# The first half step of a two-level matrix kernel by eight plain block products instead of seven, and where two token sums are made

## The reference, cut to what matters

```python
# x: (2, 2048, 512) fp32; wi[e], swi[k]: 512 x 2048; wo[e], swo[k]: 2048 x 512
s0 = relu(x @ swi[0]) @ swo[0]
s1 = relu(x @ swi[1]) @ swo[1]
eo = relu(x @ wi[type_label]) @ wo[type_label]      # one expert for each batch entry
w  = softmax(relu(concat(eo[:, 0], s0[:, 0], s1[:, 0]) @ g1) @ g2)
x  = x + eo * w0 + s0 * w1 + s1 * w2
x  = x + (x @ W[cat_ids] + b[cat_ids])
```

## Time and profile before

| | |
|---|---|
| median of three runs | 1970.01 us |
| profiled execution, device time | 1970.03 us |
| its span, first to last instruction | 1968.2 us |
| mean granted clock of TensorE | 0.994 of full |
| PE busy | 1938.7 us (99%) |
| DVE busy | 1338.0 us (68%) |
| ACT busy | 982.4 us (50%) |
| POOL busy | 525.2 us (27%) |

### The profile page before, as it was taken

The page is one execution under the profiler, slowest core; times in us unless marked ns, Lnnn a source line. Parts: engine busy times, 40 slices in busy tenths (PEclk is TensorE's granted clock), DMA queues, the critical chain, the costliest instruction groups (busy, mean ns, idle before and its releaser), DMA issues.

```text
span 1968.2 us, 25213 instructions
## 1 busy us (share of the span) xinstructions
PE 1938.7 (99%) x8504; PEld 1598.9 (81%) x8504; DVE 1338.0 (68%) x1391; ACT 982.4 (50%) x1438; POOL 525.2 (27%) x399
## 2 busy tenths in 40 slices
PE   6999999998999999999999999999999999999999
PEld 5888888887888888888888888888878888888887
DVE  7888788899566565555755554579985665565556
ACT  6666766665453433344554444456655533344342
POOL 5546545553121111111211111254531111111120
PEclk8999999999999999999999999999999999999999
DMA  6776667766876666666776676678767776656652
GB/s 219 257 260 263 257 256 288 278 240 253 286 243 215 215 212 212 189 196 194 247 257 206 193 227 199 202 258 297 268 232 264 247 235 205 216 182 211 230 160 96
DMA packets 187026, 450.99 MB, mean 229 GB/s; under 512 B 16916, under 2 KB 57876, under 8 KB 180500
## 3 DMA queue, kind: packets, MB, share of 16 engines
q1 hardware_dynamic: 186900, 449.39, 67.5%
HBM read 308.81 MB, written 140.51 MB: 228 GB/s over the span
## 4 chain that ended last, share of the span: by engine, by line
PE 95%; DVE 3%; DMA 1%; issue 1%; ACT 1%; POOL 0%; SPq 0%; DVEq 0%; ACTq 0%; POOLq 0%
PE ups L1351 46%; PE rps L1351 45%; PE aps L1351 3%; DMA XT<-in_x_dram 1%; DVE XT L604 0%; DVE XL L996 0%; DMA XS<-in_x_dram 0%; DVE WU L1005 0%; DVE HT L623 0%; DVE HL L1025 0%; DVE ACC L1044 0%; ACT HH L814 0%; DVE WD L1012 0%; DVE XT L1308 0%; ACT WD L752 0%
## 5 line engine op out<-in xcount | busy, mean ns | idle before, releaser
L1351 PE MATMUL ups<-XH,WU 128*128 128x512 f32 x2688 | 891.3, 392 | 24.6 <-DVE WU L1005 9.0
L1351 PE MATMUL rps<-HH,WD 128*128 128x512 f32 x2672 | 877.5, 389 | 0.6 <-ACT rps L829 0.6
L1351 PEld LDWEIGHTS ups<-XH,WU 128*128 128x128 f32 x2688 | 508.0, 189 | 137.4 <-ACT u L774 9.5
L1351 PEld LDWEIGHTS rps<-HH,WD 128*128 128x128 f32 x2672 | 502.4, 188 | 106.1 <-DVE HL L1025 1.3
L1351 PE MATMUL ups<-XL,WU 128*128 128x512 f32 x1344 | 526.1, 391 | 0.0
L1351 PE MATMUL rps<-HL,WD 128*128 128x512 f32 x1336 | 520.3, 389 | 0.0
L623 POOL TENSOR_TENSOR HT<-hid 128x512 f32<-128x512 f32 x96 | 135.1, 1408 | 998.8 <-PE rps L1351 998.8
L1025 DVE TENSOR_TENSOR HL<-HT,HH 128x1024 fp32r<-128x1024 f32 x240 | 306.2, 1286 | 9.2 <-ACT HH L814 5.1
L1351 PEld LDWEIGHTS ups<-XL,WU 128*128 128x128 f32 x1344 | 254.1, 189 | 52.2
L1351 PEld LDWEIGHTS rps<-HL,WD 128*128 128x128 f32 x1336 | 251.3, 188 | 52.2
L1047 DVE SCALAR_TENSOR_TENSOR ACC<-rps,gw,ACC 128x1024 f32<-128x1024 f32 x126 | 161.6, 1282 | 191.7 <-PE rps L1351 191.5
(11 more groups left out here) (113 smaller groups left out, 1574.3 us busy)
## 6 DMA issues: line engine op xcount, KB each, us to landing
WU<-wu_kept SPq DMA_DIRECT2D x448, 256.0 KB, 3.3
WD<-wd_kept SPq DMA_DIRECT2D x224, 512.0 KB, 3.3
wd_kept<-WD SPq DMA_DIRECT2D x112, 512.0 KB, 3.1
wu_kept<-WU SPq DMA_DIRECT2D x32, 1024.0 KB, 4.9
wu_kept<-WU SPq DMA_DIRECT2D x32, 768.0 KB, 4.5
sums_kept<-ACC SPq DMA_DIRECT2D x28, 512.0 KB, 5.8
MB<-sums_kept SPq DMA_DIRECT2D x28, 512.0 KB, 5.6
PUR<-in_L_cond_swi_dram SPq DMA_DIRECT2D x16, 512.0 KB, 6.0
```

The lines of the kernel that those rows point to most:

```text
L1351: ins = pe.matmul(dst, stationary[a], moving[c], start=start and j == 0, stop=stop and j == 2, skip_group_check=True)
```

## The change

Half step 0 is no longer made by the seven products but by eight plain ones (`PLAIN`): each of the four output blocks is the sum of two products of raw blocks, held in the four banks of `rps`, which are idle at that time. It needs the four raw weight blocks (`first_up_high`, `first_up_low`, into the slots 0, 1, 3 and 5 of WU) and the token blocks B11, B12, B21 and B22. B12 is not an operand of the seven, so it gets high and low parts of its own in slot 4 (`first_B12_high`, `first_B12_low`), which T1's parts take over later. Four relus straight from the banks (`first_relu`) take the place of the copies and adds of half step 0.

Later supers need the seven operands of that half step all the same. So its block sums are made apart, into SR and WS (`first_up_sums` on POOL, behind `up_sums(1)`; `first_sums_high`, `first_sums_low`), and written by `keep_first_sums`. SR and WS lie where HL and HH have their slots 5 and 6, so `hidden_sum` 3 and `hidden_high` 5 and 6 of step 0 wait for them.

T1 and T4 of the first tokens are made on POOL (`token_sum(pool, 0, 2)` and `(pool, 0, 3)`), and the order of the lists up to the first step is written out anew. From m = 0 on only one thing differs: `up_low(2, 1)` stands ahead of the hidden sums of DVE.

```diff
+PLAIN = [(0, 0, 0, 0), (2, 1, 0, 3), (0, 0, 4, 1), (2, 1, 4, 2), (1, 3, 6, 1), (3, 5, 6, 2), (1, 3, 3, 0), (3, 5, 3, 3)]
+PLAIN_WEIGHTS = [(0, 0), (2, 1), (1, 3), (3, 5)]
@@ sync
+            def keep_first(late):
+                part = slice(3, 6, 2) if late else slice(0, 1)
+                sp.wait_ge(s_wlu, 4 if late else 1)
+                sp.dma_start(wu_kept[0, :, part, :, :], WU[:, part, :, :].bitcast(F32)).then_inc(s_wuk[late], 16)
...
-            keep_up(0, 0)
+            keep_first(0)
+            keep_first(1)
...
+            blocks_up(2, experts)
+            keep_up(1, 0)
+            keep_up(1, 1)
+            blocks_up(3, experts)
+            keep_up(2, 0)
+            keep_first_sums()
+            keep_down(0, 0)
+            keep_down(0, 1)
@@ gpsimd
+            def first_up_sums():
+                A11, A12, A21, A22 = (PUR[:, 0, q, :] for q in range(4))
+                pool.wait_ge(s_pu[0], 16)
+                pool.tensor_tensor(SR[:, 2, :], A21, A22, ALU.add).then_inc(s_S0, 1)
+                pool.tensor_tensor(SR[:, 0, :], A11, A21, ALU.subtract).then_inc(s_S0, 1)
...
-            up_sums(0)
-            for m in range(-1, STEPS):
+            up_sums(1)
+            first_up_sums()
+            token_sum(pool, 0, 2)
+            token_sum(pool, 0, 3)
+            up_sums(2)
+            hidden_sum(pool, 0, 0, 0)
+            hidden_sum(pool, 0, 0, 1)
+            down_sums(0, False)
+            down_sums(0, True)
+            hidden_sum(pool, 0, 0, 2)
@@ scalar
+            def first_relu(p):
+                c = PLAIN[p][3]
+                dst = HT[:, 1, 0, :] if c == 3 else hid[:, c, 0, :]
+                act.wait_ge(s_up, p)
+                act.activation(dst, rps[c // 2][:, c % 2, :], ACT.Relu).then_inc(s_relu, 1)
...
+            first_product(1)
+            seventh_product(1)
             token_high(0, 4)
...
+            chain(1)
+            token_high(0, 5)
+            up_high(2, 0)
@@ vector
+            for k in range(4):
+                first_up_low(k)
+            first_B12_low()
+            token_low(0, 6)
+            token_low(0, 3)
             token_sum(dve, 0, 0)
             token_sum(dve, 0, 1)
             token_low(0, 1)
-            up_low(0, 1)
+            up_low(1, 0)
             token_low(0, 2)
...
@@ tensor
+            def plain(p):
+                _, slot, i, c = PLAIN[p]
+                if i == 4:
+                    pe.wait_ge(s_b12l, 1)
+                else:
+                    pe.wait_ge(s_xlo, x_index(0, i) + 1)
+                pe.wait_ge(s_wlu, [q for _, q in PLAIN_WEIGHTS].index(slot) + 1)
...
+            for p in range(len(PLAIN)):
+                plain(p)
+            for i in range(PRODUCTS):
+                up(1, i)
```

More of the change, by code:

```diff
@@ L502, in _ @@
             cats = [sp.value_load(ids[0:1, 2 + b:3 + b], min_val=0, max_val=W.shape[0] - 1) for b in range(NBATCH)]
-            for m in range(-1, STEPS):
+            blocks_up(2, experts)
[6 more added lines that the diff above has]
+            keep_down(0, 1)
+            for m in range(STEPS):
                 N, d = m + 1, m
@@ L611, in hidden_sum @@
                 eng.wait_ge(s_dn, before + (3, 2, 4, 5)[which] + 1)
+            elif which == 3:
+                eng.wait_ge(s_wsl, 2)
             if which == 0:
@@ L1153, in category_low, with first_up_low, first_B12_low, first_sums_low @@
                                   ALU.subtract).then_inc(s_wcl, 1)
-            token_low(0, 0)
-            token_sum(dve, 0, 2)
-            up_low(0, 0)
+            def first_up_low(k):
+                src, dst = PLAIN_WEIGHTS[k]
+                dve.wait_ge(s_whu, k + 1)
+                dve.tensor_tensor(WU[:, dst, 1, :], PUR[:, 0, src, :], WU[:, dst, 0, :].bitcast(F32),
+                                  ALU.subtract).then_inc(s_wlu, 1)
+            def first_B12_low():
+                dve.wait_ge(s_b12h, 1)
+                dve.tensor_tensor(XL[:, 4, :], XS[:, 1, :], XH[:, 4, :].bitcast(F32), ALU.subtract).then_inc(s_b12l, 1)
+            def first_sums_low(late):
+                part = slice(2 * late, 2 * late + 2)
+                dve.wait_ge(s_wsh, late + 1)
+                dve.tensor_tensor(WS[:, part, 1, :], SR[:, part, :], WS[:, part, 0, :].bitcast(F32),
+                                  ALU.subtract).then_inc(s_wsl, 1)
+            token_low(0, 0)
+            for k in range(4):
+                first_up_low(k)
+            first_B12_low()
+            token_low(0, 6)
+            token_low(0, 3)
             token_sum(dve, 0, 0)
@@ L1160, in _ @@
             token_low(0, 1)
-            up_low(0, 1)
+            up_low(1, 0)
             token_low(0, 2)
[L1163 to L1167, removed]
+            up_low(1, 1)
+            token_low(0, 4)
+            token_low(0, 5)
+            up_low(2, 0)
+            block_22(1)
+            hidden_low(0, 0)
+            block_21(1)
+            first_sums_low(0)
+            first_sums_low(1)
+            down_low(0, 0)
+            down_low(0, 1)
+            up_low(2, 1)
+            for m in range(STEPS - 1):
                 N, d = m + 1, m
@@ L1380, in up @@
                 ins.then_inc(s_up, 1)
+            def plain(p):
[5 more added lines that the diff above has]
+                pe.wait_ge(s_wlu, [q for _, q in PLAIN_WEIGHTS].index(slot) + 1)
+                begun = c in [q[3] for q in PLAIN[:p]]
+                for q in range(2):
+                    cols = slice(q * P, (q + 1) * P)
+                    toks = slice(q * TB, (q + 1) * TB)
+                    ins = product(rps[c // 2][:, c % 2, :], (WU[:, slot, 0, cols], WU[:, slot, 1, cols]),
+                                  (XH[:, i, toks], XL[:, i, toks]), q == 0 and not begun, q == 1 and begun)
+                if p > 0:
+                    ins.then_inc(s_up, 1)
             def down(N, p):
```

157 lines of the change are left out of this document (102 added, 55 removed).

## The result

The changed kernel takes 1965.09 us (median of 8 runs, 1963.94 to 1966.25), the kernel before beside it 1970.14 (8 runs). The ratio is 0.9972, with an interval of 0.9962 to 0.9982. I had forecast 1967.9, a gain of 2.1 us; it is 5.0. The profiled execution took 1965.15 us, its span is 1963.3.

What follows compares the result with a forecast made beforehand. The prediction took the start to be bound by turns of DVE and POOL; summed step by step, they bring up(2,6) 2.1 us earlier: 1970.03 - 2.1 = 1967.9 us (50%), range 1964.8 to 1970.6.

Steps and rivals of the forecast that it cites:

- The mechanism of the start: Up to up(2,6): DVE and POOL take turns, and the sum of both engines' turns sets the end; 2.1 us gained.
- DVE's row of turns: Start, up to T1 and T4: eight POOL turns (4.8 us) plus DVE's own (6.35) run from 13.2 to 24.35.
- T4 alone on POOL: A POOL sum of 1024 columns, which no row showed: taken as 2.35 us, against 1.1 on DVE.
- step 2: Start, to the end of T4: DVE's low parts until 13.2, turns until 24.35, T4 done at 29.05, up(1,4) waiting 4.6 us.
- everything behind it moves with it: After up(2,6), at 61.31 us before: the rest of the kernel shifts by the 2.1 us gained there.
- The larger gain: Rival at up(2,4): u is ready when down(0,0) ends, so up(2,4) comes 5.0 us earlier, total 1965.0 us; 24%.
- my own bound: Whole kernel: 0.2%, 3.9 us, is what a measurement can tell from no change; faster means under 1966.1 us.
- The POOL sums: Rival: T1 and T4 on POOL cost 2 x 1.95 us more, delaying block_22(1) and on, total 1971.8 us; 8%.
- The loads: Rival: kept copies of plain weights go ahead of B21 and PUR 1, starting the turns up to 1.5 us later, 1969.4; 4%.
- the clock full at the first plain product: First plain product, about 7.4 us: PE stands only 1.2 us before it, so the clock stays at 2.4 GHz.

Runs made afterwards that it cites:

- experiment 2: The changed kernel with T1 and T4 back on DVE, behind the last low part of half step 1: 1963.74 us, ratio 0.9964.
- experiment 4: The changed kernel with `up_low(2, 1)` behind the three hidden sums of DVE again, as before the change: 1966.47 us, ratio 0.9978.
- experiment 7: The changed kernel with DVE's T3 of the second super waiting for POOL's first hidden sum of step 11: 1966.23 us, ratio 0.9979.
- experiment 9: The changed kernel with T1 and T4 back on DVE and `up_low(2, 1)` back behind the hidden sums: 1965.14 us, ratio 0.9968.
- experiment 10: The changed kernel with 12 more matmuls of ones ahead of the first plain product: 1965.49 us, ratio 0.9972.
- experiment 5: The kernel before, unchanged, run and profiled once more: 1969.81 us, one run.
- experiment 6: The kernel before with POOL's first hidden sum of step 11 waiting for T3 of the second super: 1968.83 us, ratio 0.9994.
- experiment 1: The changed kernel with the sums made apart placed ahead of `up_sums(1)` on POOL: 1964.37 us, ratio 0.9966.
- experiment 3: The changed kernel with the sums made apart ahead of `up_sums(1)` on POOL, and T1 and T4 on DVE: 1961.65 us, ratio 0.9949.
- experiment 8: The kernel before with only `up_low(2, 1)` moved ahead of the three hidden sums of DVE: 1968.10 us, ratio 0.9988.

## Why the prediction was partly wrong

**The mechanism of the start held.** Its steps, as predicted and as measured, in us:

| step | predicted | measured |
|---|---|---|
| first plain product | 7.43 | 7.61 |
| `up_sums(1)` starts on POOL | 12.2 | 11.68 |
| DVE's row of turns, from its first to its last instruction | 13.2 to 24.35 | 12.54 to 23.68 |
| T4 alone on POOL | 2.35 | 2.35 |
| T4 ends | 29.05 | 28.25 |
| up(1,4) | 30.2 | 29.42 |
| up(1,6) | 36.65 | 35.71 |
| up(2,3) | 46.8 | 45.77 |
| up(2,4), waiting for u | 53.15 | 52.17 |
| up(2,6) | 59.2 | 58.18 |

The distances hold to 0.15 us: the row of turns was 11.14 long instead of 11.15, up(1,6) to up(2,3) 10.06 instead of 10.15, up(2,3) to up(2,4) 6.40 instead of 6.35, from there to up(2,6) 6.01 instead of 6.05.

**First failed term: where the row of turns begins, 0.7 us.** In step 2 I took the landing of B21 as 3.39 + 7.5 = 10.9 and had B12, B22 and B21 done on DVE at 13.2. B21 came at 10.28, ACT copied it from 10.30 on, and DVE went on to T3 at 12.54. In the changed kernel and in experiments 2, 4, 7, 9 and 10, T3 starts 2.26 us behind B21's landing each time, so that landing sets the row's start. PUR 1 came 0.6 us early too (11.54 instead of 12.17), but DVE wasn't through before 12.5, so this decided nothing. XS 1 landed at 7.73 where I had 8.4, and B12's low part started at 8.84 and not at 9.5. Everything behind moved up with the row: by 0.7 at its start, 0.8 at T4's end, 0.9 at up(1,6) and 1.0 from up(2,3) on; the 0.3 that came on the way are the small errors of the turns. Most of that is chance: experiment 5 has 10.2 for B21 in the kernel before, unchanged. Over the twelve profiles it lies between 10.21 and 10.88 in the kernels without the plain products and between 9.89 and 10.28 in those with them, so a small part may belong to the change; no experiment separates the two. The profile that I read had the latest landing of all, and I took its landings as values without a spread.

**Second failed step: "everything behind it moves with it".** I showed one window of 100 us without a wait behind the start and put nothing for the other 1800 us. But PE's waits behind the start are 9.7 us in six places in the same trace. One of them, at 461 us, hung on who comes first by 0.14 us. It vanished, and 1.4 us with it; experiments 6 and 7 show the mechanism from both sides. In every kernel with the plain products the two instructions start within 0.02 us and DVE has the turn (7 of 7 profiles without the wait of experiment 7; in experiments 1 to 4 POOL's row even starts 0.01 to 0.02 earlier, so rows this close don't tell who is first). In every one without them POOL starts 0.13 to 0.14 earlier (3 of 3 without that of experiment 6). What shifts the two against each other, 400 us behind the edit, isn't settled. The order of `up_low(2, 1)` isn't it: experiment 8 has it and keeps the wait.

The gain between the two profiles exceeded the forecast by 2.8 us: 0.9 in the start, 1.4 around 454 us, and 0.5 of chance.

**Third, chance:** the clock and small gaps behind 480 us (0.3) and the late starts at 411 us (0.2). They differ as much between two executions of the kernel before.

**The rivals.** The larger gain (1965.0) gave nearly the measured time, by luck, since its mechanism didn't come: u was not ready when down(0,0) ended, PE waited 2.02 us for it (2.25 forecast), and T1 and T4 weren't cheaper than 2.35. By my own bound (under 1966.1) the result is faster, for which I had 0.24. The POOL sums at twice 2.17 fell with that price. The loads didn't come late, they came early. I had the clock full at the first plain product; it was at half from 7.5 to 10.9 us, after PE had stood 2.1 us (I had 1.2 for the whole wait, it was 2.2, because the matmuls of ones ended at 5.4 instead of 6.3), and experiment 10 shows that this cost nothing at up(2,6).

## What to carry to other kernels

Where two engines take turns at a memory, add up the turns of both in the order of their lists: it gave each distance of the start within 0.15 us. Count too the turns that a shifted instruction meets at its new place (experiment 1). The landing of a load among other loads has a spread, here 1 us over twelve profiles. Before saying that all behind a shifted stretch shifts with it, list every wait of the engine that sets the end, and look at each for a pair of instructions of DVE and POOL that start within 0.2 us of each other: their order may flip. And in a change of several parts, try each alone: here one part cost about 2 us of what the others gave, and without it, with one more exchange on POOL, the kernel is at 1961.65 instead of 1965.09 (ratios 0.9949 and 0.9972).

## What the runs showed that I had not expected

- A tie is dear. POOL asking 0.14 us ahead of DVE makes a DVE sum of 1024 columns take 2.31 us instead of 1.22; DVE ahead makes POOL's sum of 512 take 2.36 instead of 1.36. The Trainium skill (SBUF — State Buffer, section "SBUF: two separate sides") says that whichever of the two starts first has the pair of ports for the whole instruction. The trace agrees: POOL's ended at 453.76 + 1.36 = 455.12, and DVE's, 1.09 later, at 456.21.
- The clock fell at 7.5 us, when PE had stood 2.1 us, just before it began again. With matmuls of ones in the gap it did not fall. Windows of the changed kernel's start: length, PE busy, clock, DMA share, GB/s.

```profile
6.00:7.00 1.00, 0.00 (x0) 1.00 1.00 320
7.00:8.00 1.00, 0.39 (x1) 0.75 0.99 397
8.00:9.00 1.00, 1.00 (x3) 0.50 1.01 401
...
10.00:11.00 1.00, 1.00 (x4) 0.54 1.06 422
11.00:12.00 1.00, 1.00 (x6) 1.00 1.12 356
```

- Behind the same wait of 3.6 us, the stretch at the half level differs between executions of the same kernel: a mean granted clock of 0.86 or 0.93 over 25 us, and 3.0 to 4.5 us lost behind the two waits in one execution, over all kernels run here. With the 1.2 us that the start shows between executions, it is part of the spread of the runs of one kernel, 1.6 to 4.7 us.
- A POOL sum of two fp32 operands of 1024 columns without DVE in its way took 2.35 us, on the line of 0.72 for 256 and 1.29 for 512.
